# Second cross attention of a two-layer decoder: the copies of the probabilities that TensorE turns move from VectorE, ahead of a step's maximum, to ScalarE, between a step's exponentials and its first plane

## The reference

```python
xn = _layernorm(x, ln_gamma, ln_beta)
q = (xn @ w_q).reshape(B, SQ, NUM_HEADS, DIM_HEAD)
kv = context @ w_kv
scores = jnp.einsum('bqhd,bkhd->bhqk', q * SCALE, k)
attn = jax.nn.softmax(scores, axis=-1)
out = jnp.einsum('bhqk,bkhd->bqhd', attn, v).reshape(B, SQ, INNER)
out = out @ w_out + b_out
return out * jnp.tanh(gate[0])
```

## Time and profile before

| | |
|---|---|
| median of three runs | 1888.37 us |
| the profiled execution | 1887.34 us, of which the span of its instructions 1885.4 us |
| busy in the span | PE 88%, DVE 84%, ACT 67%, POOL 49% |
| copies `keep_turned` | 96, median 692 ns each |
| loop of the second cross attention | first maximum at 609.4 us, last at 1679.2 us |

### The profile page before, as it was taken

How to read it: one execution, slowest core, us unless ns; L and a number is a source line. 1 busy time by engine, 2 the same in 40 slices (tenths; PEclk the granted TensorE clock), 3 DMA queues, 4 the chain that set the end, 5 groups by cost and what they waited for, 6 DMA issues and landing times. The chain is left out here.

```text
span 1885.4 us, 34643 instructions
## 1 busy us (share of the span) xinstructions
PE 1659.2 (88%) x10393; PEld 1012.3 (54%) x10393; DVE 1575.7 (84%) x2911; ACT 1271.5 (67%) x2106; POOL 924.1 (49%) x723
## 2 busy tenths in 40 slices
PE   4887998799958799999999999999999999994997
PEld 2554665677733344544554554454455455453886
DVE  4985785777758999999999999999999999975887
ACT  2442332777745887887888888788788888864554
POOL 3640111263344857466574765746657466421333
PEclk9997998799978999999999999999999999997998
DMA  5202884322100799988988889898898888984231
GB/s 186 98 1 84 323 331 188 91 46 44 46 33 18 157 198 181 199 183 176 206 173 183 193 182 193 176 198 184 176 207 173 188 187 182 186 135 122 47 80 28
DMA packets 632266, 281.85 MB, mean 149 GB/s; under 512 B 601852, under 2 KB 606236, under 8 KB 631452
## 3 DMA queue, kind: packets, MB, share of 16 engines
q1 hardware_dynamic: 632204, 281.10, 65.0%
HBM read 129.02 MB, written 1.05 MB: 69 GB/s over the span
## 5 line engine op out<-in xcount | busy, mean ns | idle before, releaser
L2237 DVE SCALAR_TENSOR_TENSOR xa_h<-xa_psum,xa_rinv,xa_h 128x500 f16<-128x500 f32 x672 | 452.8, 729 | 0.9 <-ACT xa_h L2445 0.7
L2445 ACT ACTIVATE xa_h<-xa_psum,xa_rinv 128x1000 f16<-128x1000 f32 x448 | 370.6, 880 | 51.9 <-DVE xa_rinv L2228 51.6
L2429 ACT ACTIVATE xa_psum<-xa_psum,xa_bias,unscale_s 128x1500 f32<-128x1500 f32 x224 | 352.4, 1573 | 7.4
L2073 PE MATMUL xa_psum<-xa_c_hi,xa_q_hi 128*128 128x500 f16 x672 | 257.4, 383 | 52.5 <-DVE xa_h L2237 48.0
L2217 DVE TENSOR_REDUCE xa_psum<-xa_psum 128x1 f32<-128x1000 f32 x224 | 269.3, 1202 | 13.4 <-PE xa_psum L2075 13.3
L2098 PE MATMUL xa_psum<-xa_prT,xa_n_hi 128*128 128x512 f16 (+1 forms) x768 | 270.8, 353 | 3.7 <-issue 1.6
L2100 PE MATMUL xa_psum<-xa_prT,xa_n_lo 128*128 128x512 f16 (+1 forms) x768 | 270.6, 352 | 0.0
L2099 PE MATMUL xa_psum<-xa_prT,xa_n_hi 128*128 128x512 f16 (+1 forms) x768 | 270.6, 352 | 0.0
L2074 PE MATMUL xa_psum<-xa_c_lo,xa_q_hi 128*128 128x500 f16 x672 | 252.7, 376 | 0.0
L2075 PE MATMUL xa_psum<-xa_c_hi,xa_q_lo 128*128 128x500 f16 x672 | 252.4, 376 | 0.0
L1939 POOL TENSOR_SCALAR xa_ctxT<-xa_ctxT,scales 128x1500 f32<-128x1500 f32 x31 | 126.2, 4072 | 168.8 <-DMA xa_ctxT<-in_ctxT 168.8
(11 more groups left out here) (325 smaller groups left out, 3645.4 us busy)
## 6 DMA issues: line engine op xcount, KB each, us to landing
ctxN<-in_ctxP SPq DMA_DIRECT2D x16, 1536.0 KB, 9.4
xa_ctxP<-in_ctxP SPq DMA_DIRECT2D x32, 768.0 KB, 4.5
ctxT<-in_ctxT SPq DMA_DIRECT2D x16, 1500.0 KB, 6.4
xa_ctxT<-in_ctxT SPq DMA_DIRECT2D x32, 750.0 KB, 4.7
moe_spread<-weight_rows SPq DMA_DIRECT2D x16, 1024.0 KB, 8.6
xa_prT<-xa_h SPq DMA_TRANSPOSE x192, 5.5
up<-in_F_up SPq DMA_DIRECT2D x1, 2048.0 KB, 7.8
down<-in_F_down SPq DMA_DIRECT2D x1, 2048.0 KB, 11.9
```

The source lines that it names most:

```text
L2073: nc.tensor.matmul(out, qh, c_hi[:, b, a:z], start=True, stop=False)
L2237: nc.vector.scalar_tensor_tensor(low, psum[:, bank + a:bank + z, 0:W], rinv[:, s % 2, :], high, ALU.mult, ALU.subtract).then_inc(h2_ready, 1)
L2429: nc.scalar.activation(psum[:, bank:bank + 3, 0:W], psum[:, bank:bank + 3, 0:W], ACT.Exp, bias=bias[:, s % 2, :], scale=k.unscale_s[:, :], ...
L2445: nc.scalar.activation(h[:, H_SLOT[s], 0, a * W:z * W].rearrange("p (a c) -> p a c", c=W), psum[:, bank + a:bank + z, 0:W], ACT.Identity, ...
```

## The change

`keep_turned` is defined for ScalarE and no longer for VectorE. It waits for the same semaphore `turn_ready` and raises the same `turn_kept`; the copy is an ACTIVATE with the function Copy in place of a copy of VectorE. In a step's order it stands behind `exponentials` of that step and ahead of evacuation and `high_part`. Behind the last pair, ScalarE makes the three copies of unit 11 in a row. Two waits of the start of the loop, which guarded the first write to `prT`, move with it. TensorE's, GpSimd's and SyncE's instructions and waits are not touched.

```diff
--- before.py
+++ after.py
@@ -2207,7 +2207,6 @@
         def _(dve):
             open_sems(dve, NU, two_ready, max_ready, total_ready, rinv_ready)
             open_sems(dve, NL * NU, h2_ready)
-            open_sems(dve, NR, *turn_kept.values())
             t.open_vector(dve)
 
             def maximum(i, s):
@@ -2237,13 +2236,6 @@
                     nc.vector.scalar_tensor_tensor(low, psum[:, bank + a:bank + z, 0:W], rinv[:, s % 2, :], high,
                                                    ALU.mult, ALU.subtract).then_inc(h2_ready, 1)
 
-            def keep_turned(i, u, r):
-
-                dve.wait_ge(turn_ready[u], this(i, r + 1, NR))
-                nc.vector.tensor_copy(
-                    prT[:, P_SLOT[u], :, :].rearrange("p (x k) c -> p k x c", x=2)[:, r * KT // NR:(r + 1) * KT // NR, :, :],
-                    turn_bank).then_inc(turn_kept[u], 1)
-
             def residual(i):
 
                 dve.wait_ge(y_ready, this(i))
@@ -2255,9 +2247,6 @@
             def step(i, s, first=False, end=False):
                 if s or not first:
                     inverse(*unit(i, s - 1))
-                at = turn_at(*unit(i, s - 1))
-                if at and (s >= UPS or not first):
-                    keep_turned(*at)
                 if s == RESIDUAL and not first:
                     residual(i - 1)
                 maximum(i, s)
@@ -2370,16 +2359,11 @@
                     x_low(2)
                 if s == 2:
                     x_low(3)
-                    dve.wait_ge(tok_stored, CHUNKS)
-                    dve.wait_ge(xT_ready, CHUNKS)
 
             def epilogue():
                 i = PAIRS - 1
                 inverse(i, NU - 1)
-                keep_turned(i, TURNED[1], 0)
                 low_part(i, NU - 1)
-                keep_turned(i, TURNED[1], 1)
-                keep_turned(i, TURNED[1], 2)
                 residual(i)
                 t.vector_normalise(dve, i, 0)
                 t.vector_logits(dve, i, 0, psum[:, 7, 0:E])
@@ -2392,7 +2376,15 @@
             open_sems(act, NU, exp_ready, bias_scaled)
             open_sems(act, 2 * NU, h1_ready)
             open_sems(act, NG, on_kept)
+            open_sems(act, NR, *turn_kept.values())
             t.open_scalar(act)
+
+            def keep_turned(i, u, r):
+
+                act.wait_ge(turn_ready[u], this(i, r + 1, NR))
+                nc.scalar.activation(
+                    prT[:, P_SLOT[u], :, :].rearrange("p (x k) c -> p k x c", x=2)[:, r * KT // NR:(r + 1) * KT // NR, :, :],
+                    turn_bank, ACT.Copy).then_inc(turn_kept[u], 1)
 
             def evacuate(i, g):
                 units, b = GROUP_UNITS[g], g // 2
@@ -2448,6 +2440,9 @@
 
             def step(i, s, first=False, end=False):
                 exponentials(i, s)
+                at = turn_at(*unit(i, s - 1))
+                if at and (s >= UPS or not first):
+                    keep_turned(*at)
                 if s == STORE and not first:
                     t.scalar_store(act, i - 1, 0, psum[:, 7, 128:256])
                 at = evacuation_at(i, s)
@@ -2507,8 +2502,11 @@
                     keep_features(CHUNKS - 2)
                 if s == 1:
                     keep_features(CHUNKS - 1)
+                    act.wait_ge(tok_stored, CHUNKS)
 
             def epilogue():
+                for r in range(NR):
+                    keep_turned(PAIRS - 1, TURNED[1], r)
                 for s in range(UPS):
                     at = evacuation_at(PAIRS, s)
                     if at:
```

## The result

The changed kernel takes 2138.83 us (median of four runs, 2132.94 to 2142.34), the kernel before 1888.17 (four runs). The ratio is 1.132, with a 95% interval of 1.130 to 1.134: 251 us slower. The profiled execution took 2142.34 us.

What follows compares the result with a forecast made beforehand. The prediction took the loop to be bound by a ring of maximum, exponentials, inverse and next maximum. The profiled 1887.34 us plus 203.8 for stalls gave 2091, plus 56 for the clock 2147 us, own range 2110 to 2185.

Steps and rivals of the forecast that it cites:

- The copy on ScalarE: Each moved copy, from PSUM to fp16, was to take 1.11 us on ScalarE, against 0.69 on VectorE.
- Where the copy lands, and who stands behind it: TensorE waits, next scores queued behind: three rounds of `turn` (steps 11, 0, 1), `project` (2), `outputs` (7), store transpose (12).
- The stalls without the clock: Second cross attention's loop: 90 stalls, less what steps without VectorE's copy gain, +203.8 us in all.
- The terms for `turn` and the store: Steps 11, 0 and 1 each +2.23 us for `turn`; step 12 +2.48 us for the store's transpose.
- That of `project`: Step 2, where `project` waits for the copy: 7.19 us against 4.39, +2.80.
- that of `outputs`: Step 7, where `outputs` waits for the copy: 7.93 us against 4.62, +3.31.
- The clock: TensorE's clock falls to 1.2 GHz after half of the 90 stalls, 1.25 us each: +56 us.
- What was costed at nothing: Later `high_part`, DMA transposes, two moved waits at the start, the last pair's three copies: no time added.
- The clock holds: Rival: stalls as worked out, TensorE's matmuls stay at 0.37 to 0.39 us; 2091 us, chance 0.24.
- Every stall is followed by a fall: Rival: TensorE's clock falls after each of the 90 stalls; 2203 us, chance 0.17.
- half of it is hidden: Rival: only the rounds of `turn` stall, 44 stalls fewer; 1965 us, or 1983 with half slow; chance 0.04.
- Faster: Rival: TensorE does not stand at the waits, ScalarE bounds copying steps; 36 us less, 1852 us, chance 0.03.

Runs made afterwards that it cites:

- the filled kernel: The changed kernel with 10 or 13 more zero-weight matmuls on TensorE ahead of each stall: 2081.60 us, ratio 1.103 to the kernel before.
- the first experiment: The changed kernel with its copies still on ScalarE, moved ahead of their step's exponentials: 1898.87 us, 1.0064 times the kernel before (1852 expected).

## Why the prediction was right

Forecast 2147 us, measured 2138.8.

- *The copy on ScalarE.* 1.11 us taken, 1.013 measured, 9 us less over 90 stalls. It is still longer than VectorE's 0.69. The prediction cited the Trainium skill, Advanced Engine Details and Errata, The Read-Write Bubble, for ScalarE as the engine nearer to PSUM; the shorter copy that it would have made of this did not come.
- *Where the copy lands, and who stands behind it.* Right in all six places, and shown by experiments: the copy earlier on the same engine (240 and 282 us back), the copy late on the other engine (203 us lost), and the scores ahead of the wait (187 us back with the copy as late as ever).
- *The stalls without the clock.* +203.8 forecast, 192.5 measured by the kernel whose gaps are filled (2081.60 - 1889.06, the median of before beside it). From the table, 15 x (2 x 1.98 + 3.41 + 2.29) + 14 x 3.10 + 16 x 1.98 - 32 x 0.61 - 15 x 0.57 = +191.9 with step 11 taken as the two others. The terms for `turn` and the store were 0.2 too large, of which the copy is 0.1. That of `project` was 0.3 too small and that of `outputs` 0.1, and step 13 returned to 4.44 and not only to 4.65.
- *The clock.* +56 forecast, 57.2 measured (2138.83 - 2081.60). Half of 90 stalls were to be followed by a fall, 44 are. The half was a choice between the two bounds and not worked out, so the fit is partly luck. So is its split: I had 0.8 us for steps 11, 0 and 1 and 1.7 for 2, 7 and 12, and step 12 was never slowed and step 11 in all pairs but the first, by 1.4 us.
- *What was costed at nothing* stayed so: no step outside the table moved by more than 0.1 us in its median. From the first maximum to the last the traces take 1069.8 us before and 1320.0 after: 250 of the 255 us by which the two profiled executions differ lie in the loop.
- *The rivals.* "The clock holds" was 2091 and is the filled kernel, 2082. "Every stall is followed by a fall" is out with 44 of 90, and "half of it is hidden" with stalls in all six places. "Faster" asked that TensorE not stand at the waits; it stood at every one. The sum of the first experiment, near the same 1852 us, failed for another reason: there the copy stands ahead of the exponentials and can't fill the reciprocal's 0.48 us.

What stays open is which stalls bring the clock down. In this trace, none of the 27 stalls that stand directly behind a stall with a fall has one itself (the prediction expected this of some neighbours): 9 in step 1, 3 in step 2 and 15 in step 12. That would give step 12 its none, once step 11 always has one. But it is no rule. With only unit 4 changed, 2 of the 11 stalls of step 12 behind a slowed step 11 had a fall, and in the four pairs in which step 11 had none, step 12 had none either. I made no run for it.

## What to carry to other kernels

Moving a copy to an engine with free time is no gain by itself; what decides is whether it still ends before its consumer needs it. Find the instruction that waits for it, what is queued behind that instruction, and where the new place ends relative to when the waiter arrives. Here one step earlier or later on the same engine is the difference between 31 us gained and 251 lost. And moved work fills an engine's waiting time only if it stands at that wait in the engine's order. The 0.48 us for the reciprocal took in the copy behind the exponentials, and stayed idle with the copy ahead of them. A sum of an engine's busy times is a lower bound for a step, and the step is longer where such a wait stays open.

## What the runs showed of the hardware

- TensorE's granted clock fell from 1.00 to 0.50 at 44 of the 90 stalls, with gaps of 2.4 to 2.8 us. With the copy late on VectorE it also fell at many gaps of 2.1 us. It fell between 0.6 us ahead of the restart and 1.3 behind it (0.9 behind at 1190.2, 1.3 in the earlier trace rows), and each slow stretch lasted 3.4 us. Adding 993 matmuls that do nothing left gaps of 0.3 to 0.7 us and no fall in the loop behind the first pair, and took 57 us off.

The Trainium skill, TensorE: Matmul & The Clock Gate, What's actually happening, describes the full clock as released by activity; the filled kernel agrees, 1.00 against 0.93.

- TensorE restarts 0.06 us behind the copy for `turn` (1197.09 to 1197.15), but 0.38 us behind it for `project`. In the timeline, step 2 of a pair:

```profile
1203.06 1.01 ACT L2385 ACTIVATE xa_prT<-xa_psum 128x1024 f16<-128x1024 f16 x1
...
1204.45 0.27 PE L2057 MATMUL xa_psum<-xa_x_hi,kq_hi 128*128 x1 [2.83 <-ACT xa_prT L2385]
```

The same 0.37 to 0.40 us stand in all 14 pairs of the filled kernel, where the clock is full, so the clock is not the reason. `project` has further waits behind the one for the copy, where `turn` has none; `outputs` has one more and restarts 0.13 us behind the copy. That these waits make the 0.3 us is only argued. It is the size by which the term of `project` was too small.
